# High parts first: finer waits and reordered products on TensorE in a post-norm transformer layer

## What is computed

```python
x = L0_attn_x
x = _layernorm(x + _L0_attn_ref(x, L0_attn_Wqkv, L0_attn_Wout), axis=-1)
x = _layernorm(x + _L0_ffn_ref(x, L0_ffn_w_gate, L0_ffn_w_up, L0_ffn_w_down), axis=-1)
# attention: qkv = x @ Wqkv; softmax(q k / 4 + slopes * rel, causal) @ v; out @ Wout
# feed-forward: h = silu(x @ wg.T) * (x @ wu.T); h @ wd.T, weights = int / 127
```

## Time and profile before

| | |
|---|---|
| median of 3 runs | 2004.0 us (2002.14 to 2005.53) |
| the profiled execution's own time | 2002.88 us |
| its span, first to last instruction | 2001.1 us |
| mean granted TensorE clock | 0.986 of 2.4 GHz |
| TensorE matmuls | 1896.9 us busy, 18468 |
| VectorE | 1500.7 us busy, 75% |
| ScalarE | 1208.4 us busy, 60% |
| GpSimd | 1091.3 us busy, 55% |

### The profile page before, as it was taken

How to read it: one execution, slowest core, us unless ns; L and a number is a source line. 1 busy time by engine, 2 the same in 40 slices (tenths; PEclk the granted TensorE clock), 3 DMA queues, 4 the chain that set the end, 5 groups by cost and what they waited for, 6 DMA issues and landing times.

```text
span 2001.1 us, 46915 instructions
## 1 busy us (share of the span) xinstructions
PE 1896.9 (95%) x18468; PEld 1457.8 (73%) x18468; DVE 1500.7 (75%) x2521; ACT 1208.4 (60%) x1999; POOL 1091.3 (55%) x2052
## 2 busy tenths in 40 slices
PE   5889999999999999999999999999999999999986
PEld 4556777777777777777777777777777777777666
DVE  5567787777787777878777878777778777777745
ACT  1655666566666666666666666666666656666653
POOL 0234655555565555565555565555566556556565
PEclk7999999999999999999999999999999999999998
DMA  5464544444444444445445454444454444444320
GB/s 202 148 198 138 171 150 146 162 157 144 158 157 152 154 152 158 149 153 168 139 150 172 139 168 153 144 162 160 133 170 157 143 158 157 151 156 141 109 76 27
DMA packets 164860, 299.29 MB, mean 150 GB/s; under 512 B 33920, under 2 KB 84864, under 8 KB 152064
## 3 DMA queue, kind: packets, MB, share of 16 engines
q1 hardware_dynamic: 164448, 295.24, 45.1%
q10 hardware_dynamic: 192, 1.05, 0.2%
HBM read 175.64 MB, written 119.54 MB: 148 GB/s over the span
## 4 chain that ended last, share of the span: by engine, by line
PE 69%; DVE 12%; ACT 10%; POOL 7%; issue 2%; DMA 1%; SPq 0%; POOLq 0%; DVEq 0%; ACTq 0%
PE pair L574 68%; ACT probs L795 6%; DVE row_max L874 4%; DVE row_max L877 4%; DVE x1t_lo L862 2%; POOL probs L993 2%; POOL attn_lo L1013 2%; ACT pv_t L803 2%; POOL attn L1008 2%; POOL h_lo L1000 1%; ACT x1t_hi L775 1%; PE pair L577 1%; DVE row_max L879 0%; DMA probs<-L_attn_Wqkv 0%; DVE staged_lo L862 0%
## 5 line engine op out<-in xcount | busy, mean ns | idle before, releaser
L795 ACT ACTIVATE probs<-pair 128x1024 f32<-128x1024 f32 x640 | 620.7, 1030 | 320.9 <-PE pair L574 320.4
L993 POOL TENSOR_SCALAR_AFFINE_SELECT probs<-probs 128x256 f32<-128x256 f32 (+1 forms) x896 | 380.1, 440 | 650.9 <-ACT probs L795 646.7
L1000 POOL TENSOR_TENSOR h_lo<-h_fulls,h_hi 128x256 fp32r<-128x256 f32 x384 | 276.9, 743 | 129.4 <-ACT h_hi L827 127.9
L574 PE MATMUL pair<-probs,v_ones 128*32 128x512 f32 (+3 forms) x4096 | 328.5, 439 | 4.4 <-ACT probs L795 1.5
L574 PE MATMUL pair<-q_rows,k_rows 64*128 64x512 f32 (+3 forms) x2048 | 315.3, 365 | 8.3 <-ACT probs L795 0.8
L877 DVE TENSOR_REDUCE row_max<-pair 128x2 f32<-128x1024 f32 x256 | 312.4, 1220 | 12.7 <-PE pair L574 8.0
L574 PE MATMUL pair<-k_rows,q_rows 63*128 63x512 f32 (+3 forms) x2048 | 296.9, 347 | 23.4 <-DVE row_max L877 15.2
L879 DVE TENSOR_REDUCE row_max<-pair 128x8 f32<-128x1024 f32 x256 | 311.8, 1218 | 0.0
L574 PEld LDWEIGHTS pair<-k_rows,q_rows 63*128 63x128 f32 x2048 | 165.2, 186 | 168.6 <-DVE row_max L877 81.4
L874 DVE TENSOR_REDUCE row_max<-pair 128x4 f32<-128x1024 f32 x128 | 156.7, 1224 | 123.8 <-PE pair L574 123.8
L819 ACT ACTIVATE h_fulls<-pair 128x256 f32<-128x256 f32 x384 | 145.0, 378 | 153.7 <-PE pair L574 149.9
(11 more groups left out here) (89 smaller groups left out, 3411.8 us busy)
## 6 DMA issues: line engine op xcount, KB each, us to landing
q_rows<-bounce SPq DMA_DIRECT2D x192, 256.0 KB
k_rows<-bounce SPq DMA_DIRECT2D x192, 256.0 KB
bounce<-staged_hi SPq DMA_DIRECT2D x128, 256.0 KB, 2.5
bounce<-staged_lo SPq DMA_DIRECT2D x128, 256.0 KB, 2.8
pv_bounce<-pv_t SPq DMA_DIRECT2D x128, 256.0 KB, 2.0
x_sb<-L_attn_x SPq DMA_DIRECT2D x32, 512.0 KB, 4.2
attn<-pv_bounce SPq DMA_DIRECT2D x64, 256.0 KB
recips<-recip_bounce SPq DMA_DIRECT2D x64, 256.0 KB
```

Source lines behind the costliest of these rows:

```text
L574: return tensor.matmul(o, lhs, rhs, start=start, stop=stop, skip_group_check=True, **kw)
L795: scalar.activation(probs[g][:, tile, :, :], pair[:, :, :], ACT.Exp, scale=scale).then_inc(s_exp, 1)
L993: made = pool.affine_select(out=diagonal, in_=diagonal, compare_op=ALU.is_ge, fill=0.0, base=0, pattern=[[0, diagonal.shape[1]], [1, P]], ...
L1000: pool.tensor_tensor(h_lo[:, m, :], h_full[(n_split_h[step] - 1) % H_BUFFERS][:, :], h_hi[:, m, :].bitcast(F32), ALU.subtract).then_inc(s_ ...
```

## The change

Waits and order on TensorE alone are changed; the number of matmuls, their operands and the list of steps stay, and so does the work of all other engines.

- x1: the wait for the normalised rows is made once before row block 0 (for blocks 0 and 1) and once before row block 2 (for 2 and 3).
- project: waits for the high part of both halves, makes hi hi, then lo (weights) hi, then, each behind a wait for its half's low part, hi lo.
- out: waits for the high part; the loop over t becomes the inner one, so that all four hi hi and four lo hi matmuls of both row blocks come ahead of the four with the low part, which wait for it half by half.
- gate_up: waits for the high parts; the matmuls with the low part wait for it half by half. The order stays.
- down: for each m, waits for the high part of h before its two matmuls and for the low part before the other two. The order stays.

```diff
+                        if kind == "x1" and t % 2 == 0:
+                            e.wait_ge(s_norm1, 2 * n_norm1["norm1", n, t])
...
-                    e.wait_ge(s_lo, n_lo["split_lo", "x", u // 2, 1])
+                    e.wait_ge(s_hi, n_hi["split_hi", "x", u // 2, 1])
...
+                        if xx is xt_lo:
+                            e.wait_ge(s_lo, n_lo["split_lo", "x", u // 2, c])
...
-                    e.wait_ge(s_attn_lo, n_attn_lo["attn_lo", 2 * b + 1])
+                    e.wait_ge(s_attn_hi, n_attn_hi["attn_hi", 2 * b + 1])
...
-                    for t in range(2):
-                        for n, (w, a, c) in enumerate(terms):
+                    for n, (w, a, c) in enumerate(terms):
+                        if a is attn_lo:
+                            e.wait_ge(s_attn_lo, n_attn_lo["attn_lo", 2 * b + c])
+                        for t in range(2):
...
-                                      w[:, c, :], n == 0, n == 5)
+                                      w[:, c, :], (n, t) == (0, 0), n == 5)
...
-                    e.wait_ge(s_lo, n_lo["split_lo", "x1", b, 1])
+                    e.wait_ge(s_hi, n_hi["split_hi", "x1", b, 1])
...
+                            if xx is x1t_lo:
+                                e.wait_ge(s_lo, n_lo["split_lo", "x1", b, c])
...
-                        e.wait_ge(s_split_h, n_split_h["split_h", b, part, m])
-                        for n, hh in enumerate((h_hi, h_lo)):
+                        for n, (hh, made_h) in enumerate(((h_hi, s_h_hi), (h_lo, s_split_h))):
+                            e.wait_ge(made_h, n_split_h["split_h", b, part, m])
```

More of the change, by code:

```diff
@@ L597, in _ @@
                     else:
-                        e.wait_ge(s_norm1, blocks * (n + 1))
                         source = x1[n % 2]
                     for t in range(blocks):
+                        if kind == "x1" and t % 2 == 0:
+                            e.wait_ge(s_norm1, 2 * n_norm1["norm1", n, t])
                         made = turn(bank[:, t * P:(t + 1) * P], source[:, t, c * P:(c + 1) * P])
@@ L607, in _ @@
                     col = side * dim + (u % 2) * P
-                    e.wait_ge(s_lo, n_lo["split_lo", "x", u // 2, 1])
+                    e.wait_ge(s_hi, n_hi["split_hi", "x", u // 2, 1])
                     e.wait_ge(s_split_w, SPLIT_W[u % 2 + 1])
-                    terms = [(w, xx, c) for w, xx in ((wqkv_hi, xt_hi), (wqkv_hi, xt_lo), (wqkv_lo, xt_hi)) for c in range(kd)]
+                    terms = [(w, xx, c) for w, xx in ((wqkv_hi, xt_hi), (wqkv_lo, xt_hi), (wqkv_hi, xt_lo)) for c in range(kd)]
                     for n, (w, xx, c) in enumerate(terms):
+                        if xx is xt_lo:
+                            e.wait_ge(s_lo, n_lo["split_lo", "x", u // 2, c])
                         made = mm(bank, w[:, c, col:col + P], xx[:, c, :], n == 0, n == 5)
```

## The result

| | before | changed |
|---|---|---|
| median of the runs compared | 2003.07 us | 1971.58 us (1969.47 to 1973.31) |
| ratio to before, 95% interval | | 0.9836 (0.9824 to 0.9849) |
| the profiled execution's own time | 2002.88 us | 1973.31 us |
| its span | 2001.1 us | 1971.6 us |

The change takes 31.5 us off the median and 29.6 us off the profiled execution. Forecast were 26.8 us and a median of 1977, within 1969 to 1990.

The account below looks back on a forecast made before the run. The prediction took TensorE plus its standstills as the bound. Gate 10.2, output projection 7.0, start-up 4.1 and tail 5.5 us sum to 26.8 us off 2002.9, a median of 1977 us, range 1969 to 1990.

Parts of the forecast that it names:

- Gate, part 0: gate_up in part 0: a shorter standstill for x1's low part gains 0.35 us in 29 batches, 10.2 us.
- Rival 3: gate_up: the mid-stream wait vanishes, the whole 0.63 us, 8 us more gained: 1969 us, chance 0.10.
- Output projection: Output projection in part 1: its wait for attn_lo goes, net 0.25 us in 28 batches, 7.0 us.
- the alternation: Output projection with t as inner loop: 12 pairs per batch at 0.004 us cost 0.05 us.
- Projections, down, transposes, waits: Steady part: zero gain in each; some 600 added satisfied waits free, at most 1.5 us of loss.
- Start-up: Three projections and the first output projection stop waiting for low parts: 4.1 us gained, bound below 2.
- Tail: Last output projections, gate_ups and downs, with no other work around: 5.5 us gained, bound below 3.
- Pass-through: TensorE's gains reach the total time: DVE idles 1.56 us after part 0 and follows; after part 1 it is tight.
- Rivals 1 and 2: Attention: rival 1, or attention's own rhythm absorbs both steady gains, leaving 9.6 us: 1994 us, chance 0.07.
- rival 1: After part 1: VectorE, busy without a gap, takes back the output projection's 7.0 us: 1984 us, chance 0.15.
- Rival 4: Down: added waits break the stream of weight loads or cost queue slots: 2010 or 2012 us, chance 0.05.
- rival 5: Another semaphore (a bank, the row maxima) also ends the standstill, so nothing changes: 2003 us, chance 0.03.

Follow-up runs that it names:

- e1: The kernel before with the change of gate_up alone: median 1988.33 us, ratio 0.9919.
- e4: The changed kernel with gate_up's four high-part products ahead of its four low-part ones: median 1967.05 us, ratio 0.9815.
- e7: The kernel before with t as the inner loop of the output projection, its wait unchanged: 2003.23 us in one execution.
- e3: The kernel before with the changes of x1's transposes, project and down alone: median 2000.28 us, ratio 0.9986.
- e5: The changed kernel with one more satisfied wait on the second matmul of each part in down (768 more): median 1972.64 us, ratio 0.9843.
- e8: The changed kernel with a second, satisfied wait before each wait for h_lo in down (384 more): median 1971.71 us, ratio 0.9834.
- e9: The changed kernel once more, unaltered, for a side-by-side comparison: median 1972.36 us, ratio 0.9843.
- e2: The kernel before with the change of the output projection alone: median 1989.26 us, ratio 0.9926.

## Why the prediction was right, point by point

- **Gate, part 0.** Forecast 0.35 us per batch, bounded by 0.2 and 0.63; it is 0.41, and 0.43 in e1. The wait moved into mid-stream as worked out, to x1t_lo's second half. The size was a little off because the standstill there is about 0.1 us, not 0.1 to 0.2. From VectorE's end to the matmul it is 0.055 us in the changed trace; before it was 0.15 (1006.74 to 1006.89). There two semaphores stood before one load, and the trace has a wait instruction of its own between them (1006.78, 0.05 us long). Where one semaphore stood before the load, in front of out, it was 0.05 us before too (1038.83 to 1038.88). That the second semaphore is the cause is read from these rows and was not tried. Rival 3, a wait that vanishes whole, is not what this change does, but e4 does it.
- **Output projection.** Forecast 0.25, of 0.30 less 0.05 for the alternation; it is 0.32 to 0.33. The failed term is that 0.05, which e7 shows to be zero within the spread. The 1.2 us of cover in front of the low part held.
- **Projections, down, transposes, waits.** Forecast zero in the steady part, at most 1.5 us of loss from waits; e3 shows 0.015 us per period less, e5 and e8 no cost of waits.
- **Start-up.** Forecast 4.1; 2.4 in the profiled pair, 2.8 as a mean over traces with the same stretches at the lower clock, 3.4 over all. The first project starts at 9.35 us instead of 10.63 and each of the next two is 0.7 and 1.2 us nearer to the transposes before it, as said. What the sum put at nothing is what is lost between these steps, 2.1 us in the profiled pair. The wait for the stored row maxima behind the gather (0.8 us before, 2.6 us now) can be up to 1.9 us of it, which is argued and not shown. "What is late next" was asked of VectorE and not of SyncE's queue.
- **Tail.** Forecast 5.5; 6.3 in the profiled pair. The last output projections wait for the high part alone, 0.24 and 0.28 us, where 1.42 us (at 1923.86) and 1.38 us had been spent on the low part. The same stretch at the end is 158.7, 160.4 and 158.8 us in e5, e8 and e9 against 158.2 in the changed kernel's trace, so this term is known to some 2 us only.
- **Pass-through.** Rivals 1 and 2 fall by the sum of e1, e2 and e3. For rival 1 the prediction set two margins (0.1 to 0.2 us and 0.07 us) against 0.25 us; the gain was 0.32 us, and the pauses in VectorE's rows were 0.33. The mechanism was right, and that it was just enough was luck. Rival 4 falls by e5 and e8; rival 5 by the list of waits.

In total, 28 periods times 0.75 make 20.9 us where 29 x 0.35 + 28 x 0.25 = 17.2 was forecast for them: 3.7 us more. The start-up gave 1.7 us less and the tail 0.8 us more, so the profiled pair differs by 2.8 us more than forecast. The total is closer than its terms because two of their errors cancel in part, which is luck.

The last output projections, changed kernel:

```profile
1900.07 0.71 PE L574 MATMUL pair<-wout_hi,attn_hi 128*128 128x256 f32 x4 [0.24 <-ACT attn_hi L817]
...
1928.14 0.71 PE L574 MATMUL pair<-wout_hi,attn_hi 128*128 128x256 f32 x4 [0.28 <-ACT attn_hi L817]
```

## What to carry to other kernels

Where an engine bounds the kernel, measure its standstills from start to start against a twin of the same transition that waits for nothing; the idle time in brackets gave 0.38 us for a standstill that was worth 0.62, and none for one worth 0.3. A step that needs its operands one after another should wait for each where it is first used, and do first all the work that needs only the early ones: in gate, two matmuls with high parts in front of those with low parts left a loss of 0.2 us, four left none. Ask of every queue what is late next, also of the one that issues transfers.

## What the runs showed of the hardware that was not expected

- Satisfied waits on TensorE were free: 768 more on weight loads, or 384 more as instructions of their own in its queue, left down at 2.97 us.
- A late wait costs more than its standstill: in the changed kernel the matmul behind it comes 0.22 us later instead of 0.12. A wait of 0.1 us in mid-stream cost 0.21 us.
- Alternating matmuls between the two halves of a bank cost nothing in out (2.910 us against 2.924 for 24 matmuls).
- The same twelve start-up matmuls took 2.9 us in one trace (granted clock 1.00) and 5.3 us in another (0.50). One stretch of 3.4 us at 1.2 GHz more or less between 83 and 165 us went with some 2 us of start-up.
